# Narrow-head attention: scores made in rows for the maxima and again turned, from stacked high and low parts

## The chip, the cores and the metric

One core of a Trainium2 chip runs the whole network in one launch. The metric is device time in microseconds of one execution, the median of several. A profiled execution is one of them with the trace recorded.

## What is computed

x has 8 batches of 256 rows of 128 channels (2048 rows, 16 tiles of 128 rows, two tiles per batch); the context has 8 x 64 rows. Four layers follow each other, each an attention to the context and a feed-forward part. The change touches the attentions of layer 0 and layer 2, which have 16 narrow heads of 8 channels:

```python
q = split(layernorm(x) @ wq + bq)        # 16 heads of 8
k = split(ctx @ wk + bk); v = split(ctx @ wv + bv)
logits = einsum('bhqd,bhkd->bhqk', q, k) / sqrt(8) + mask * -1e9   # layer 2: no mask
out = einsum('bhqk,bhkd->bhqd', softmax(logits), v)
x = x + merge(out) @ wo + bo
```

Layer 0's mask is one 256 x 64 table for all batches and heads.

## The kernel before

The program is a row of stages (`nc.Block`). A block gives each engine (TensorE, VectorE, ScalarE, GpSimd, and SP, which issues DMAs) its own program, and ends with a barrier that all five pass together. Within a block engines meet by semaphores. Ahead of each narrow attention stand `normalise` (tag n) and, for layer 0 alone, a setup block (tag su) that turns the context and prepares masks. Then come two blocks.

`project_small` (tag p): TensorE makes K for all batches (`pk`, one 512-column product), V for all batches (`pv`) and Q in four groups of 512 rows (`pq`); ScalarE adds the biases and writes `kT_all` and `qT_all`, channels in partitions, and VectorE writes `v2_all`. SP has no program here.

`attend_small` (tag t) goes tile by tile, 16 tiles, in a loop of four with lags: step t makes scores of tile t, transposes those of t-1, multiplies those of t-2 with V, turns and projects the output of t-3, and adds it to x for t-4.

- GpSimd: once per batch the keys spread over 16 heads with zeros between (`kbd`, L352), per tile a copy of its q (`qs`, L357) and the output bias.
- TensorE: scores as two fp32 products of 512 columns (L374); eight transposes of 128x128 (L382) once the exponentials are there; the turn of the normalised output (L389); eight products with `vaug`, V with columns of ones for the denominators (L397); the output projection (L403). An fp32 product is two records in the trace.
- VectorE: in layer 0 scale and mask over 1024 scores per row (L467); maxima (L472); subtraction (L474); division by the denominators (L481, L483); addition to x (L460).
- ScalarE: exponentials (L435); copy of the transposed weights out of PSUM (L426); V placed in `vaug` (L421); the turned output (L431).

Ahead of the loop VectorE fills `vaug` (L443, L451), for which ScalarE waits, but not TensorE. During layer 0's attention SP loads the weights of the next parts (L2547).

Of the kernel before, what the change touches and what calls it, by code (L numbers as in the profile page):

```python
# [268 lines left out]
def project_small(nc, tag, w, zT, ctx2T, ident, qT_all, kT_all, v2_all):  # L269

    with ExitStack() as stack:
        m = Memory(nc, stack, tag)
        pq = [m.ps(f"pq{i}") for i in range(2)]
        pk = m.ps("pk")
        pv = m.ps("pv", 1024)
        q_done, q_out, k_done, v_done = m.sem("q_done"), m.sem("q_out"), m.sem("k_done"), m.sem("v_done")
        block = stack.enter_context(nc.Block())

        @block.tensor
        def _(pe):  # L280
            nc.tensor.matmul(pk[:, :].rearrange("p (b k) -> p b k", k=KEYS), w["wk"][:, :], ctx2T[:, :, 0, :],
                             start=True, stop=True).then_inc(k_done, 1)
            for b in range(B):
# [4 lines left out]
            for g in range(GROUPS):  # L288
                if g >= 2:
                    pe.wait_ge(q_out, g - 1)  # L290
                nc.tensor.matmul(pq[g % 2][:, :], w["wq"][:, :], zT[:, g * 512:(g + 1) * 512],
                                 start=True, stop=True).then_inc(q_done, 1)

        @block.scalar
        def _(act):
            act.wait_ge(k_done, 1)
            nc.scalar.activation(kT_all[:, :], pk[:, :], ACT.Identity, bias=w["bk"][:, 0:1])
            for g in range(GROUPS):
                act.wait_ge(q_done, g + 1)
                nc.scalar.activation(qT_all[:, g * 512:(g + 1) * 512], pq[g % 2][:, :], ACT.Identity,  # L300
                                     bias=w["bq"][:, 0:1]).then_inc(q_out, 1)

        @block.vector
        def _(dve):
            dve.wait_ge(v_done, 1)
# [4 lines left out]
def attend_small(nc, tag, x, w, qT_all, kT_all, v2_all, ident, headmask, scale, neg=None, loads=None):  # L310
# [2426 lines left out]
```

## Time and profile before

| | us |
|---|---|
| median of 3 executions | 1593.37 |
| lowest and highest | 1592.81, 1596.17 |
| the profiled execution | 1598.73 |
| its span in the trace | 1596.8 |
| layer 0: last K of the projection to last addition | 24.7 to 131.7 |
| layer 2: the same | 905.1 to 998.8 |

In the span TensorE is busy 1283.8 us (80%), its weight loads 1032.2, VectorE 1024.7 (64%), ScalarE 734.5 (46%), GpSimd 620.8 (39%). The share of an engine is an average over stages with different limits; the two stages in question are read from the timeline.

### The profile page before, as it was taken

How to read it: one execution, taken by the hardware profiler on the slowest of the kernel's cores; microseconds unless marked ns; L12 is line 12 of the kernel's file. 1: busy time of each engine (PE TensorE's matmuls, PEld its weight loads, DVE VectorE, ACT ScalarE, POOL GpSimd, SP SyncE). 2: the span in 40 equal slices, each digit the busy share in tenths (PEclk: the TensorE clock that was granted, in tenths of full speed). 3: DMA queues.
4: the chain of work that ended last, by engine and by line, in shares of the span. 5: the costliest groups of instructions: out<-in, count | busy, mean ns of one | idle time of the engine just before them, and what ended most of it. 6: DMA issues, size and time to landing. Idle time of an engine off the chain costs nothing. (4 is left out here: it accounts for less than half of the span.)

```text
span 1596.8 us, 24399 instructions
## 1 busy us (share of the span) xinstructions
PE 1283.8 (80%) x7148; PEld 1032.2 (65%) x7148; DVE 1024.7 (64%) x2047; ACT 734.5 (46%) x1260; POOL 620.8 (39%) x598
## 2 busy tenths in 40 slices
PE   4896669997997899721997499699946659999997
PEld 2673459987664599720886267588833438787875
DVE  3885678887324276660665466677768767667675
ACT  2443446665332554430654254455523325455553
POOL 1311634431000133245233131389844116676665
PEclk9996779999898899955999599699976669999998
DMA  3500011110000000131111100133202025343333
GB/s 89 143 0 1 0 41 36 39 39 5 1 0 0 20 1 0 60 112 55 35 48 32 44 1 0 45 97 97 95 19 103 1 60 125 109 130 115 126 115 104
DMA packets 69931, 85.64 MB, mean 54 GB/s; under 512 B 14282, under 2 KB 40269, under 8 KB 69850
## 3 DMA queue, kind: packets, MB, share of 16 engines
q1 hardware_dynamic: 67250, 79.94, 17.3%
q0 software_dynamic: 2272, 4.24, 0.8%
q10 hardware_dynamic: 336, 0.59, 0.2%
q8 instruction: 34, 0.56, 0.1%
q14 instruction: 39, 0.32, 0.1%
HBM read 69.98 MB, written 8.92 MB: 49 GB/s over the span
## 5 line engine op out<-in xcount | busy, mean ns | idle before, releaser
L2356 POOL TENSOR_TENSOR e_h<-e_h,e_gate 128x512 f32<-128x512 f32 x128 | 187.8, 1484 | 145.8 <-DVE e_h L2408 89.9
L2413 DVE TENSOR_TENSOR e_h_low<-e_h,e_h_high 128x512 fp32r<-128x512 f32 x132 | 117.8, 893 | 75.6 <-ACT e_h_high L2343 75.4
L2343 ACT ACTIVATE e_h_high<-e_h 128x512 fp32r<-128x512 f32 x132 | 83.5, 633 | 97.8 <-POOL e_h L2356 90.1
L228 PE MATMUL n_ps_t<-ident,n_zn 128*128 128x128 f32 x128 | 34.4, 433 | 90.5 <-DVE n_zn L167 82.7
L2408 DVE TENSOR_TENSOR e_h<-e_s,e_ps_b 128x512 f32<-128x512 f32 x132 | 89.4, 678 | 13.1 <-ACT e_s L2328 8.7
L1001 PE MATMUL u_ps_o<-u_vaug,u_pT 128*128 128x72 f32 x768 | 96.9, 269 | 0.0
L1001 PEld LDWEIGHTS u_ps_o<-u_vaug,u_pT 128*128 128x128 f32 x768 | 93.3, 192 | 0.0
L2328 ACT ACTIVATE e_s<-e_ps_a 128x512 f32<-128x512 f32 x132 | 77.7, 589 | 31.5 <-PE e_ps_a L1364 28.4
L228 PEld LDWEIGHTS n_ps_t<-ident,n_zn 128*128 128x128 f32 x128 | 23.9, 224 | 98.2 <-DVE n_zn L167 78.3
L932 POOL TENSOR_TENSOR u_kbd<-u_keys,groupmask 96x512 fp32r<-96x512 f32 x60 | 62.8, 1067 | 62.4 <-DMA u_keys<-s_k 37.2
L1028 ACT ACTIVATE u_sm<-u_sm 128x512 f32<-128x512 f32 x96 | 60.6, 631 | 54.5 <-DVE u_sm L1060 53.9
L1058 DVE TENSOR_REDUCE u_mx<-u_ps_s 128x2 f32<-128x512 f32 (+1 forms) x96 | 66.2, 690 | 20.0 <-PE u_ps_s L983 18.5
L1804 POOL DMA_INDIRECT sorted_y<-e_y,e_zb x39 | 37.8, 970 | 88.7 <-DVE e_y L2009 88.7
L1060 DVE TENSOR_TENSOR u_sm<-u_ps_s,u_mx 128x512 f32<-128x512 f32 x96 | 66.4, 692 | 7.1
L374 PE MATMUL t_ps_s<-t_kbd,t_qs 128*128 128x512 f32 x128 | 64.6, 632 | 6.5 <-POOL t_qs L357 6.5
L558 POOL MEMSET t_vbd<- 128x1024 f32 x1 | 1.0, 951 | 170.9 <-POOLq L495 170.9
L1580 ACT ACTIVATE e_s<-e_ps_a 128x512 f32<-128x512 f32 x64 | 38.3, 598 | 57.9 <-PE e_ps_a L1364 57.9
L397 PE MATMUL t_ps_o<-t_vaug,t_pT 128*128 128x72 f32 x512 | 64.2, 281 | 0.0
L397 PEld LDWEIGHTS t_ps_o<-t_vaug,t_pT 128*128 128x128 f32 x512 | 63.1, 201 | 0.0
L571 POOL TENSOR_TENSOR t_sm<-t_sm,t_den 128x1024 f32<-128x1024 f32 x16 | 30.4, 1901 | 82.3 <-DVE t_den L683 82.3
L1024 ACT ACTIVATE u_pT<-u_ps_t 128x512 f32<-128x512 f32 x96 | 57.0, 594 | 7.7 <-PE u_ps_t L989 6.0
L1362 PE MATMUL e_ps_y<-e_h_high,ed_low 128*128 128x512 f32 x132 | 52.9, 401 | 8.4 <-DVE e_y L2417 5.4
(439 smaller groups left out, 3901.3 us busy)
## 6 DMA issues: line engine op xcount, KB each, us to landing
e_gate<-gates_by_expert SPq DMA_DIRECT2D x256, 128.0 KB, 3.0
e_gate<-gates_by_expert SPq DMA_DIRECT2D x32, 256.0 KB, 3.4
w_raw<-in_L1w SPq DMA_DIRECT2D x24, 256.0 KB, 4.2
u_qs<-s_q SPq DMA_DIRECT2D x16, 192.0 KB, 2.6
u_keys<-s_k SPq DMA_DIRECT2D x8, 384.0 KB, 3.5
w_w<-in_L2w SPq DMA_DIRECT2D x24, 128.0 KB, 2.7
sorted<-blank SPq DMA_DIRECT2D x1, 2535.0 KB, 17.6
e_zb<-sorted SPq DMA_DIRECT2D x13, 195.0 KB, 2.5
```

What stands on the lines that cost most here:

```text
L374: last = nc.tensor.matmul(ps_s[p][:, h * 512:(h + 1) * 512], qs[p][:, :], kbd[r // 2][:, 8 * h:8 * h + 8, :].rearrange("p a b -> p (a b)") ...
L397: last = nc.tensor.matmul(ps_o[:, a * NA:(a + 1) * NA], pT[p][:, j, :], vaug[vb][:, a, pair * NA:(pair + 1) * NA], start=pair == 0, stop=p ...
L932: return eng.tensor_tensor(kbd[:, HG * g:HG * (g + 1), kb * P:(kb + 1) * P], keys[:, kb, g, :].unsqueeze(1).broadcast_to([ROWS, HG, P]), g ...
L1001: last = nc.tensor.matmul(ps_o[par][:, a * NA:(a + 1) * NA], pT[(r - 3) % 2][:, i, :], vaug[kb][:, a, own * NA:(own + 1) * NA], start=own ...
L1028: nc.scalar.activation(sm[r % 3][:, :], sm[r % 3][:, :], ACT.Exp, scale=scale).then_inc(p_ready, 1)
L1058: nc.vector.tensor_reduce(mx[r % 2][:, 0:heads], s3, X, ALU.max)
L1060: nc.vector.tensor_tensor(sm[r % 3][:, :].rearrange("p (h k) -> p h k", h=heads), s3, mx[r % 2][:, 0:heads].unsqueeze(2).broadcast_to([P, ...
L2328: nc.scalar.activation(s[c % 3][:, :], ps_a[c % 3][:, :], ACT.Silu).then_inc(s_ready, 1)
L2343: nc.scalar.activation(h_parts[k % 3][0][:, :], h[k % 3][:, :], ACT.Copy).then_inc(high_ready, 1)
L2356: nc.gpsimd.tensor_tensor(h[c % 3][:, :], h[c % 3][:, :], gate[pair % SLOTS][:, :], ALU.mult)\
L2408: nc.vector.tensor_tensor(h[c % 3][:, :], s[c % 3][:, :], ps_b[c % 3][:, :], ALU.mult)\
L2413: nc.vector.tensor_tensor(h_parts[k % 3][1][:, :], h[k % 3][:, :], h_parts[k % 3][0][:, :], ALU.subtract).then_inc(low_ready, 1)
```

## The change

**A stacked form of q and k** (new class `Stacked`). q and k are kept as a high part (fp32r) and a low part (what is left). In four subsets of four heads (32 channels), the stacked `q` holds in rows 0 to 95 high, high, low and the stacked `k` high, low, high, so that one fp32r product over 96 rows gives the score but for low times low. Rows 96 to 127 take the maxima of 16 heads, high and low part; the spread keys have -1 there at their own head (`takes`).

**project_small** computes the parts (ScalarE the high ones, VectorE the low ones), and SP copies them to their rows, 32 partitions at a time. Q is made ahead of V, in four PSUM banks.

**attend_small** goes by batches, eight and three rounds of lag, written out without a loop. Per batch: scores in rows (96 stacked rows) into two banks, maxima from there; the maxima split in two parts and turned by a product with the identity; ScalarE writes them in rows 96 to 127 of `st.q` for all four subsets; scores again, now with keys in the partitions and 256 queries in the columns, maxima included; the exponential goes from PSUM to `pT`, with no subtraction, no transposes and no copy. The mask of layer 0 is added by a product of its high and low parts with a stacked identity, ahead of each bank's scores. VectorE's preparation now also zeroes `mxs` and fills rows 96 to 127 of three `kbd` tiles, and TensorE waits for it.

```diff
+def project_small(nc, tag, w, zT, ctx2T, st, v2_all):
+        @block.sync
+            def restack(out, src, cols, row, there):
+                for s in range(SUBSETS):
+                    sp.dma_start(out[row:row + 32, s, cols].bitcast(F32), src[32 * s:32 * s + 32, cols].bitcast(F32))\
+                        .then_inc(there, 16)
+            every = slice(0, B * KEYS)
+            sp.wait_ge(k_high_ready, 1)
+            restack(st.k, st.k_high, every, 0, st.k_there)
+            restack(st.k, st.k_high, every, 64, st.k_there)
+            sp.wait_ge(k_low_ready, 1)
+            restack(st.k, st.k_low, every, 32, st.k_there)
+            for g in range(GROUPS):
+                cols = slice(g * 512, (g + 1) * 512)
+                sp.wait_ge(q_high_ready, g + 1)
+                restack(st.q, st.q_high, cols, 0, st.q_there[g])
+                restack(st.q, st.q_high, cols, 32, st.q_there[g])
+                sp.wait_ge(q_low_ready, g + 1)
+                restack(st.q, st.q_low, cols, 64, st.q_there[g])
...
+            def scores(b, t):
+                for h in range(2):
+                    wait(pe, mx_used, n - 1)
+                    if mask is not None:
+                        nc.tensor.matmul(ps_s[h][:, :], mask[0][:, t * P:(t + 1) * P], mask[1][:, :],
...
+                    for i in range(2):
+                        last = nc.tensor.matmul(ps_s[h][:, i * PAIR:(i + 1) * PAIR],
+                                                st.q[0:ROWS, s, b * PAIR + t * P:b * PAIR + (t + 1) * P],
+                                                kbd[b % 3][0:ROWS, s, :, :].rearrange("p h k -> p (h k)"),
...
+            def turned_scores(b, s):
+                if s == 0:
+                    pe.wait_ge(m_rows, b + 1)
+                wait(pe, p_ready, n - RING + 1)
...
+                for pair in range(2):
+                    last = nc.tensor.matmul(bank[:, pair * PAIR:(pair + 1) * PAIR],
+                                            kbd[b % 3][:, s, 2 * pair:2 * pair + 2, :].rearrange("p h k -> p (h k)"),
+                                            st.q[:, s, cols(b)], start=mask is None, stop=True, skip_group_check=True)
...
+            pe.wait_ge(zeroed, 1)
...
+            def exponentials(b, s):
+                act.wait_ge(st_done, n + 1)
+                nc.scalar.activation(pT[b % 2][:, 2 * s:2 * s + 2, :].rearrange("p a c -> p (a c)"), ps_t[n % RING][:, :],
+                                     ACT.Exp, scale=scale).then_inc(p_ready, 1)
...
+                if 0 <= b - 1 < B:
+                    place_values(b - 1)
+                    exponentials(b - 1, 0)
+                    exponentials(b - 1, 1)
+                    exponentials(b - 1, 2)
+                if 0 <= b - 2 < B:
+                    out_T(TPB * (b - 2))
+                if 0 <= b - 1 < B:
+                    exponentials(b - 1, 3)
...
+            for i in range(3):
+                last = nc.vector.tensor_copy(kbd[i][ROWS:P, :, :, :].rearrange("p s h k -> p (s h) k"),
+                                             takes[ROWS:P, :].unsqueeze(2).broadcast_to([P - ROWS, HEADS, KEYS]))
             last.then_inc(zeroed, 1)
```

SP's queue between the first loads and those of layer 0's attention. Before, the two batches of loads follow each other:

```order
L2547 DMA ctx_nat<-in_ctx 64x8x128
L98 UNCONDITIONAL_BRANCH
L341 UNCONDITIONAL_BRANCH [waits barrier_Pool_Activation_PE_DVE_SP_release]
L2547 DMA L0fwqkv<-in_L0fwqkv 128x384
L2547 DMA L0fwo<-in_L0fwo 128x128
```

Now the projection block stands between them, with these rows (the last four come four times, once per group of q):

```order
L98 UNCONDITIONAL_BRANCH
L304 UNCONDITIONAL_BRANCH [waits barrier_Pool_Activation_PE_DVE_SP_release]
L308 DMA a_k<-a_k_high 32x512 [waits p0_k_high_ready]
L308 DMA a_k<-a_k_high 32x512 x7
L308 DMA a_k<-a_k_low 32x512 [waits p0_k_low_ready]
L308 DMA a_k<-a_k_low 32x512 x3
L308 DMA a_q<-a_q_high 32x512 [waits p0_q_high_ready]
L308 DMA a_q<-a_q_high 32x512 x7
L308 DMA a_q<-a_q_low 32x512 [waits p0_q_low_ready]
L308 DMA a_q<-a_q_low 32x512 x3
```

Sixty DMAs were put ahead of the barrier into the attention, and the loads behind it.

TensorE in layer 0's attention, one tile in the steady part. Before:

```order
L374 MATMUL t_ps_s<-t_kbd,t_qs 128x512 [waits t0_s_used,t0_q_ready]
L374 MATMUL t_ps_s<-t_kbd,t_qs 128x512
L382 MATMUL t_ps_t<-ident,t_sm 128x128 [waits t0_pT_ready,t0_p_ready]
L382 MATMUL t_ps_t<-ident,t_sm 128x128 x7
L389 MATMUL t_ps_w<-ident,t_on 128x128 [waits t0_x_done,t0_on_ready]
L397 MATMUL t_ps_o<-t_vaug,t_pT 128x72 [waits t0_pT_ready]
L397 MATMUL t_ps_o<-t_vaug,t_pT 128x72 x7
L403 MATMUL t_ps_w<-L0wo,t_onT 128x128 [waits t0_onT_ready]
```

Now the second half of a round (one batch), from the second tile's scores in rows (L423 the mask, L427 the scores; L449 and L453 the same turned):

```order
L423 MATMUL t0_ps_s0<-wide_eye,hidesT 128x512 [waits t0_mx_used]
L427 MATMUL t0_ps_s0<-t0_kbd0,a0_q 128x256 x2
L423 MATMUL t0_ps_s1<-wide_eye,hidesT 128x512 [waits t0_mx_used]
L427 MATMUL t0_ps_s1<-t0_kbd0,a0_q 128x256 x2
L466 MATMUL t0_ps_o<-t0_vaug1,t0_pT1 128x72 [waits t0_p_ready,t0_on_ready]
L466 MATMUL t0_ps_o<-t0_vaug1,t0_pT1 128x72 [waits t0_p_ready] x7
L449 MATMUL t0_ps_t1<-hidesT,wide_eye 128x512 [waits t0_p_ready]
L453 MATMUL t0_ps_t1<-a0_q,t0_kbd2 128x256 x2
L474 MATMUL t0_ps_w<-ident,t0_on0 128x128 [waits t0_x_done,t0_on_ready]
L449 MATMUL t0_ps_t2<-hidesT,wide_eye 128x512 [waits t0_p_ready]
L453 MATMUL t0_ps_t2<-a0_q,t0_kbd2 128x256 x2
L478 MATMUL t0_ps_w<-L0wo,t0_onT0 128x128 [waits t0_onT_ready]
```

The transposes are gone, scores stand twice, and between the turn of the output (L474) and its projection (L478) stands one turned score.

VectorE at the head of layer 0's attention. Before two rows of memsets stand ahead of the first scores:

```order
L443 MEMSET t_vaug 128x704 x2
L451 MEMSET t_vaug 64x2 x16
L467 SCALAR_TENSOR_TENSOR t_sm<-t_ps_s,mask 128x1024 [waits t0_s_done]
L472 TENSOR_REDUCE t_mx<-t_sm 128x16
L474 TENSOR_TENSOR t_sm<-t_sm,t_mx 128x1024
```

Now:

```order
L561 MEMSET t0_zeros 128x256
L563 MEMSET t0_vaug0 128x704
L563 MEMSET t0_vaug1 128x704
L566 CAST t0_mxs0<-t0_zeros 128x256
L571 MEMSET t0_vaug0 64x2 x8
L566 CAST t0_mxs1<-t0_zeros 128x256
L571 MEMSET t0_vaug1 64x2 x8
L573 CAST t0_kbd0<-takes 32x1024
L573 CAST t0_kbd1<-takes 32x1024
L573 CAST t0_kbd2<-takes 32x1024
L580 TENSOR_REDUCE t0_mx0<-t0_ps_s0 128x8 [waits t0_nat_done]
```

Three key tiles, two tiles for the maxima and a tile of zeros were put ahead, and over the scores only the maxima are left.

## Rows read from the trace of the kernel before

**Rows 1.** Busy time by stretches: length, then PE, PEld, DVE, ACT, POOL, granted clock, DMA share, GB/s.

```profile
930.00:990.00 60.00, 59.59 (x398) 47.28 (x396) 41.87 (x65) 31.37 (x51) 17.03 (x27) 1.00 0.00 0
...
118.00:124.00 6.00, 5.26 (x27) 5.12 (x27) 0.64 (x3) 1.88 (x3) 0.00 (x0) 0.62 0.00 0
```

**Rows 2.** Timeline, layer 2's attention, TensorE: start, us, engine, line, op, names, count.

```profile
956.36 1.88 PE L374 MATMUL t_ps_s<-t_kbd,t_qs 128*128 128x512 f32 x4
...
958.08 1.04 PE L382 MATMUL t_ps_t<-ident,t_sm 128*128 128x128 f32 x8
...
959.07 1.90 PE L397 MATMUL t_ps_o<-t_vaug,t_pT 128*128 128x72 f32 x16
...
961.08 1.88 PE L374 MATMUL t_ps_s<-t_kbd,t_qs 128*128 128x512 f32 x4
```

**Rows 3.** Timeline, layer 0's attention, VectorE: the mask step of two tiles, eight apart.

```profile
68.87 1.23 DVE L467 SCALAR_TENSOR_TENSOR t_sm<-t_ps_s,mask 128x1024 f32<-128x1024 f32 x1 [0.75 <-PE t_ps_s L374]
...
109.04 1.23 DVE L467 SCALAR_TENSOR_TENSOR t_sm<-t_ps_s,mask 128x1024 f32<-128x1024 f32 x1 [0.74 <-PE t_ps_s L374]
```

**Rows 4.** Timeline, first scores and last addition of both attentions.

```profile
34.31 5.26 PE L374 MATMUL t_ps_s<-t_kbd,t_qs 128*128 128x512 f32 x8 [3.29 <-POOL t_qs L357]
...
131.43 0.29 DVE L460 TENSOR_TENSOR x<-x,t_ps_w 128x128 f32<-128x128 f32 x1 [1.79 <-PE t_ps_w L403]
...
914.75 5.37 PE L374 MATMUL t_ps_s<-t_kbd,t_qs 128*128 128x512 f32 x8 [3.21 <-POOL t_qs L357]
...
998.49 0.29 DVE L460 TENSOR_TENSOR x<-x,t_ps_w 128x128 f32<-128x128 f32 x1 [1.34 <-PE t_ps_w L403]
```

**Rows 5.** Timeline, ScalarE in both projection blocks: K, and the last Q.

```profile
24.04 0.69 ACT L297 ACTIVATE a_kT<-p_pk,L0bk 128x512 f32<-128x512 f32 x1 [2.38 <-PE p_pk L281]
...
31.06 0.69 ACT L300 ACTIVATE a_qT<-p_pq,L0bq 128x512 f32<-128x512 f32 x1 [0.17 <-PE p_pq L291]
...
904.44 0.69 ACT L297 ACTIVATE a_kT<-p_pk,L2bk 128x512 f32<-128x512 f32 x1 [2.38 <-PE p_pk L281]
...
911.58 0.69 ACT L300 ACTIVATE a_qT<-p_pq,L2bq 128x512 f32<-128x512 f32 x1 [0.17 <-PE p_pq L291]
```

**Rows 6.** Timeline, SP's queue: 1 row, 128 rows; then twice 96 rows of 4 bytes.

```profile
11.73 0.34 SPq L2547 DMA_DIRECT2D starts<-in_starts  x1
12.12 0.39 SPq L2547 DMA_DIRECT2D mask<-in_mask  x1
...
32.87 0.42 SPq L2547 DMA_DIRECT2D L0fqn<-in_L0fqn  x1
33.33 0.43 SPq L2547 DMA_DIRECT2D L0fkn<-in_L0fkn  x1
```

**Rows 7.** Timeline, fp32r products: 512 columns twice; then 256, 128, 256.

```profile
760.24 0.39 PE L1837 MATMUL e_ps_b<-w_high,e_z_low 128*128 x1
760.47 0.40 PE L1838 MATMUL e_ps_b<-w_low,e_z_high 128*128 x1
...
761.56 0.33 PE L1858 MATMUL e_ps_y<-w_down,e_h_high 128*128 x1
761.73 0.22 PE L1859 MATMUL e_ps_y<-w_down,e_h_low 128*128 x1
761.79 0.33 PE L1858 MATMUL e_ps_y<-w_down,e_h_high 128*128 x1
```

**Rows 8.** Timeline, VectorE: a 128x1024 step inside SBUF; the memsets of V.

```profile
19.30 0.69 DVE L2594 TENSOR_SCALAR neg<-mask 128x1024 bf16<-128x1024 uint8 x1
...
32.23 1.39 DVE L443 MEMSET t_vaug<- 128x704 f32 x2 [3.57 <-PEq L271]
```

**Rows 9.** Groups of instructions: line, names, shapes, count, busy, mean ns, idle before.

```profile
L932 POOL TENSOR_TENSOR u_kbd<-u_keys,groupmask 96x512 fp32r<-96x512 f32 x60 | 62.8, 1067 | 62.4 <-DMA u_keys<-s_k 37.2
...
L1028 ACT ACTIVATE u_sm<-u_sm 128x512 f32<-128x512 f32 x96 | 60.6, 631 | 54.5 <-DVE u_sm L1060 53.9
L1058 DVE TENSOR_REDUCE u_mx<-u_ps_s 128x2 f32<-128x512 f32 (+1 forms) x96 | 66.2, 690 | 20.0 <-PE u_ps_s L983 18.5
...
L431 ACT ACTIVATE t_onT<-t_ps_w 128x128 f32<-128x128 f32 x16 | 4.4, 272 | 8.7 <-PE t_ps_w L389 8.7
```

More of the change, by code:

```diff
@@ L282, in _ @@
                              start=True, stop=True).then_inc(k_done, 1)
+            for g in range(GROUPS):
+                nc.tensor.matmul(pq[g][:, :], w["wq"][:, :], zT[:, g * 512:(g + 1) * 512],
+                                 start=True, stop=True).then_inc(q_done, 1)
             for b in range(B):
@@ L287, in _ @@
             last.then_inc(v_done, 1)
[L288 to L292, printed above, removed]
         @block.scalar
@@ new lines, in values @@
+            def values(b, t):
+                n = TPB * b + t
+                if t == 0:
+                    pe.wait_ge(v_ready, b + 1)
+                wait(pe, on_ready, n)
+                for j in range(8):
+                    a, pair = j // 4, j % 4
+                    pe.wait_ge(p_ready, 4 * b + j // 2 + 1)
+                    last = nc.tensor.matmul(ps_o[:, a * NA:(a + 1) * NA],
+                                            pT[b % 2][:, j, t * P:(t + 1) * P], vaug[b % 2][:, a, pair * NA:(pair + 1) * NA],
+                                            start=pair == 0, stop=pair == 3)
+                last.then_inc(o_done, 1)
@@ new lines, in place_values @@
+            def place_values(b):
+                wait(act, o_done, TPB * (b - 1))
+                for half in range(2):
+                    rows = slice(64 * half, 64 * half + 64)
+                    out = vaug[b % 2][rows, :, :].rearrange("p a (j c) -> p (a j) c", c=NA + 2 * HD)
+                    src = v2_all[rows, b, :].rearrange("p (j e d) -> p j e d", e=2, d=HD)
+                    last = nc.scalar.activation(out[:, :, HD * half:HD * half + HD], src[:, :, half, :], ACT.Copy)
+                last.then_inc(v_ready, 1)
@@ new lines, in add @@
+            def add(n):
+                dve.wait_ge(w_done, n + 1)
+                dve.wait_ge(bias_added, n + 1)
+                nc.vector.tensor_tensor(x[:, n, :], x[:, n, :], ps_w[:, 0:P], ALU.add).then_inc(x_done, 1)
+            for b in range(B + 3):
+                if 0 <= b - 3 < B:
+                    add(TPB * (b - 3))
+                if b < B:
+                    maxima(b, 0)
+                if 0 <= b - 2 < B:
+                    divide(TPB * (b - 2))
+                if 0 <= b - 3 < B:
+                    add(TPB * (b - 3) + 1)
+                if b < B:
+                    maxima(b, 1)
+                    split_max(b)
+                if 0 <= b - 2 < B:
+                    divide(TPB * (b - 2) + 1)
@@ L2577, in _ @@
                 last.then_inc(turned, 1)
+                pe.wait_ge(hidden, 1)
+                for t in range(TPB):
+                    last = nc.tensor.transpose(ps_m[:, t * P:(t + 1) * P],
+                                               hides[:, t, :, :].rearrange("p a k -> p (a k)"), idn)
+                last.then_inc(hides_turned, 1)
             @block.scalar
@@ L2679, in lay_out @@
          "ident": np.eye(P, dtype=np.float32),
-         "headmask": np.repeat(np.eye(HEADS, dtype=np.float32), HD, axis=0),
+         "takes": np.concatenate([np.zeros((ROWS, HEADS), np.float32)] + 2 * [-np.eye(HEADS, dtype=np.float32)]),
+         "eye2": np.tile(np.eye(KEYS, dtype=np.float32), (2, 1)),
          "groupmask": np.tile(np.repeat(np.eye(HG, dtype=np.float32), HD, axis=0), (3, 1)),
```

331 lines of the change are left out of this document (184 added, 147 removed).

## The prediction

> **What bounds the kernel now.** I read first the busy time by stretches, then the timeline of the two attentions and of the small projections in front of them, then the groups of like instructions. The change touches two stages of a chain of stages separated by barriers, so what counts is the length of each stage, not the average over the kernel.
>
> In the L2 attention TensorE is the bound: in 930 to 990 us it is busy 59.59 of 60 us at the full clock, while VectorE has 41.87 and ScalarE 31.37 [rows 1]. The reader is to see one tile there: the scores start at 956.36, the eight transposes at 958.08, the eight products with V (16 records) with the output projection behind them at 959.07, the next scores at 961.08 [rows 2]. That is 1.72 for the scores, 0.99 for the transposes with the turn of the last output, 2.01 for values and projection: 4.72 us per tile, with nothing between. In the L0 attention the same TensorE work stands in a longer round: from the mask step of one tile at 68.87 to that eight tiles later at 109.04 is 40.17, 5.02 us per tile [rows 3]; the 0.3 more is TensorE waiting for VectorE, which there has a third pass of 1.22 us over the 1024 scores.
>
> From first score to last addition the L0 body runs 34.31 to 131.72, 97.4 us, and the L2 body 914.75 to 998.78, 84.0 us [rows 4]. Sixteen periods make 80.3 and 75.5; the rest, 17.1 and 8.5, is filling and draining. L0's rest is longer because its drain falls to the half clock (0.62 granted in 118 to 124 [rows 1]).
>
> The projection stage ahead is short: K is out of ScalarE at 24.73, the last Q at 31.75; in L2 905.13 and 912.27 [rows 5]. SP has nothing to do in it.
>
> **What is removed and added on TensorE.** Per tile the fp32 scores (1.72) and the transposes (0.88 of the 0.99) go; the values and the output stay. Per batch of two tiles come 16 fp32r matmuls of 256 columns (eight in rows for the maxima, eight turned), and two small turns of the maxima. The price of a 256-column fp32r matmul: 512 columns repeat after 0.23 (760.24 to 760.47), and a 256- and a 128-column one together after 0.23 (761.56 to 761.79) [rows 7]. 384 columns at 2.4 GHz are 0.16, so about 0.035 is added to each, and 256 columns cost 0.14; I take 0.15, with 0.13 and 0.17 as ends, since the stationary side changes at every one. A round (one batch) in L2 is then 16 x 0.15 = 2.40, turned maxima 0.22, values and projections 4.02, turns of the output 0.22: 6.86 us. L0 adds eight 512-column mask matmuls at 0.235, 1.88: 8.74 us.
>
> Waits inside the round. The even tile's projection stands behind its turn and one turned score, but on ScalarE the copy that it needs is queued behind the third exponential. That exponential starts 0.2 after turned score 2 ends and takes 0.63, the copy 0.27 [rows 9]: 1.13 with the handover. TensorE covers 0.11 + 0.30 of it (0.11 + 0.53 in L0): a wait of 0.72, 0.49 in L0. The odd tile's projection waits about 0.2 in L2. Rounds: 6.86 + 0.92 = 7.78 against 2 x 4.72 = 9.44 now, and 8.74 + 0.49 = 9.23 against 10.04. Nothing else ends later: VectorE has four maxima of 0.69, 0.65 for splitting them, 1.3 for dividing, 0.6 for adding, 5.3 per round; ScalarE four exponentials of 0.63, 1.05 for the maxima rows, 0.5 and 0.55, 4.6; GpSimd spreads one batch's keys in 2.1 (two of its 96x512 products [rows 9]) and adds two biases, about 3. The smaller of these figures are estimates from the same steps of today.
>
> Eight rounds are 62.2 and 73.8. Filling (scores, four maxima, split, turn, rows of maxima, first exponential) and draining add an estimated 6, the half clock of the first matmuls 1.8 (eight records took 5.26 where the full clock takes 3.4 [rows 4]), and in L0 2 more for a part of today's slow drain (0 to 9). Bodies: L2 70.0, so **14.0 less**; L0 83.6, so **13.8 less**.
>
> **What is added in front.** Before the first score TensorE now waits for VectorE's whole preparation: besides two memsets of V (1.39 together [rows 8]) and the ones (0.5), it fills zeros (0.3), two tiles from them (0.6) and three key tiles of 32x1024. The last have no row of their own; their ends are 0.69 (128x1024 to bf16 [rows 8]) and 1.22 (128x1024 out of PSUM [rows 3]), and I take 1.1 each, near the second, because the source is a broadcast. In sum 6.3 instead of 2.1: **+4.2 per attention**, ends 2.2 and 5.
>
> The page VectorE: DVE Perf Modes of the Trainium skill (the section on 2x mode with both ports) lets an fp32 copy inside SBUF run at twice the rate; by it the three would be 0.55 each and the sum 3.3 us less over both attentions. No row here has a copy of this shape.
>
> **The restack, the largest term.** SP now issues 60 DMAs of 32 rows in each projection block, 12 for the keys and 48 for the queries, and the block ends with a barrier that waits for SP as for every engine. What an issue costs is read off SP's queue: with 96 rows of 4 bytes the next follows after 0.46 (32.87 to 33.33), with a single row after 0.39 (11.73 to 12.12) [rows 6]; size hardly matters. For 32 rows I take 0.45, nearest the 96-row case, ends 0.38 and 0.47. SP starts when the keys' high part is out, 24.83, and stays the last engine: the last query part is computed by about 32, when SP has done sixteen. 60 x 0.45 = 27.0, so the block ends at 51.8 instead of 31.75: **+20.1**; in L2 at 932.2 instead of 912.27: **+20.0**. The GpSimd copies of q per tile that go were hidden. SP's weight loads for the next layer are now queued 20 us later (from 52, their last landing by about 87), well before 132, and hide.
>
> The page DMA: Bandwidth & Descriptors of the Trainium skill says, of the sequencer's dispatch, about 50 ns (Anatomy of one DMA), and that issuing is usually small relative to the DMA (Issuing engines are not separate DMA queues). By that, 60 issues would be 3 us and the block would hardly grow. The rows above say nine times as much, and I follow them; the rule is rival A.
>
> **Small things.** The setup block now has a second turn: mask transposed, copied by ScalarE behind its three copies (which end at 21.7), VectorE's low part behind that: **+1.0** (0.4 to 1.2). One more load in the first batch hides under the first normalisation.
>
> **The sum.** +20.1 + 20.0 + 8.4 + 1.0 - 13.8 - 14.0 = **+21.7 us**. The profiled execution took 1598.7 (span 1596.8); one like it would take 1620.4. Against the median of 1593.4 it is 1615.
>
> **Rivals.** *A, the issue is cheap.* If SP issued as fast as the parts are computed, each block would grow by about 1, and the sum is 2 + 8.4 + 1 - 27.8 = -16: **1577**. Against it stand all of SP's rows; the lowest is 0.39. The point from which it decides: the projection blocks may grow by 9.2 us each, that is 0.27 per issue. 10%.
>
> *B, the two cancel.* 0.38 per issue (-8.4) and no waits inside the rounds (-11): **1596**. It needs both, and the copy behind the third exponential stands in the order written. 8%.
>
> *C, the clock.* TensorE idles some 28 us before each attention and then 12% of each round; if it stayed at 1.2 GHz, its 6.86 and 8.74 would double, about +125: **1740**. For it: the drain in L0 fell to 0.62 at a busy share of about 0.87 [rows 1]. Against it: in L2 the same start after an idle stretch rose to the full clock within 3 us, and TensorE is now as dense as in L0. A fall in some rounds only gives tens of us. 4%.
>
> *D, the change does not do what it says* (the maxima and the mask go wrong in the split): it would alter values, not the order or sizes of instructions, and so no time. It has no share of its own.
>
> **How the numbers follow.** Forecast 1615 with 78%. Its own range: issue -8.4 to +2.4, preparation -4 to +2, fp32r matmuls -5 to +5, waits in the rounds -11 to +11, L0's drain -2 to +7. Not all at one end: 1598 to 1633. The chances left out are A, C and the tails of the forecast, about 2 in 10: 1597 to 1635. A measurement of this kernel tells about 0.2% (3.2 us) from no change. Slower: the forecast, C and half of B, 0.84. Same: half of B and the low tail, 0.06. Faster: A, 0.10.
>
> **What would show it.** SP's queue full from about 24.8 to 52 with 60 issues at 0.45, TensorE and VectorE idle at its end. The first score 6 us behind the barrier. A 256-column matmul repeating after 0.15. Rounds of 7.8 and 9.2 us, with the wait before the even tile's projection put down to ScalarE. I am wrong if issues of 32 rows take under 0.3, if rounds are over 9.4 in L2 (a new bound, or the clock), or if another engine ends the projection block.

## The result and the profile after

The changed kernel takes **1660.47 us** (median of 4 executions, 1655.23 to 1673.7) against 1594.25 of the kernel before on the same chip (4 executions, 1592.81 to 1596.17): a ratio of 1.0427, interval 1.0362 to 1.0493. It is slower by 66 us, where 21.7 were forecast, and lies outside the range of 1597 to 1635. The profiled execution has a span of 1662.1 us, 65.3 more than before, at a mean granted clock of 0.841 instead of 0.877. Of the variant e7 below, two of ten executions (1605.93 and 1606.93) were slow ones, more than 1.5% above its fastest; its median and ratio are those of the other eight, and its profile is of the first of the two.

First scores and last additions of both attentions, in the timeline of the changed kernel (start, us, engine, line, op, names); they answer to [rows 4]:

```profile
71.41 0.80 PE L423 MATMUL t_ps_s<-wide_eye,hidesT 128*128 128x512 f32 x1 [40.16 <-DVE t_kbd L573]
...
151.76 0.29 DVE L606 TENSOR_TENSOR x<-x,t_ps_w 128x128 f32<-128x128 f32 x1 [1.34 <-PE t_ps_w L478]
...
968.59 1.22 PE L427 MATMUL t_ps_s<-t_kbd,a_q 96*128 96x256 f32 x4 [39.82 <-DVE t_kbd L573]
...
1062.05 0.29 DVE L606 TENSOR_TENSOR x<-x,t_ps_w 128x128 f32<-128x128 f32 x1 [1.62 <-PE t_ps_w L478]
```

Layer 0's body, first score to last addition, is 80.6 us (97.4 before), and layer 2's is 93.7 (84.0 before). But the first scores come 37.1 us later in layer 0 and 53.8 later in layer 2. The 65.3 us divide by place: +20.3 to the end of layer 0's attention, -2.5 from there to the start of layer 2's K on ScalarE (922.27 against 904.44 [rows 5]), +36.0 from K to the first scores, +9.7 in layer 2's body, +1.7 behind it.

SP's queue in the projection block of layer 0, first and last copies and the first load of the next block; it answers to [rows 6], and the x8 and x4 are numbers of issues:

```profile
25.64 5.05 SPq L308 DMA_DIRECT2D a_k<-a_k_high  x8
30.74 2.49 SPq L308 DMA_DIRECT2D a_k<-a_k_low  x4
33.27 5.02 SPq L308 DMA_DIRECT2D a_q<-a_q_high  x8
...
61.47 2.49 SPq L308 DMA_DIRECT2D a_q<-a_q_low  x4
64.59 0.34 SPq L2685 DMA_DIRECT2D L0fwqkv<-in_L0fwqkv  x1
```

Eight issues, 30.74 - 25.64 = 5.10 us later the next: 0.64 each, where the loads that follow in the same queue go at 0.39 to 0.47. Behind the barrier comes VectorE's preparation, here its timeline with one product of GpSimd (POOL) that ran beside it:

```profile
64.73 0.27 DVE L561 MEMSET t_zeros<- 128x256 f32 x1 [32.22 <-PEq L294]
...
67.50 3.85 DVE L573 CAST t_kbd<-takes 32x1024 fp32r<-32x1024 f32 x3
67.60 2.34 POOL L407 TENSOR_TENSOR t_kbd<-a_k,groupmask 96x1024 fp32r<-96x1024 f32 x1
```

The three key tiles took 3.85 us, but one by one 0.69, 2.38 and 0.94 us: the first began ahead of GpSimd's product, the other two while GpSimd was at work.

The windows of both bodies (columns as in [rows 1]: length, then PE, PEld, DVE, ACT, POOL busy, granted clock, DMA share, GB/s):

```profile
80.00:90.00 10.00, 10.00 (x58) 9.20 (x57) 4.35 (x10) 5.00 (x9) 2.72 (x3) 0.75 1.19 252
90.00:100.00 10.00, 9.72 (x76) 9.06 (x76) 5.53 (x15) 4.14 (x9) 2.71 (x3) 1.00 0.40 61
...
1010.00:1020.00 10.00, 9.79 (x47) 9.49 (x45) 4.08 (x10) 3.47 (x6) 2.72 (x3) 0.50 0.00 1
1020.00:1030.00 10.00, 9.79 (x44) 9.26 (x44) 3.22 (x10) 3.23 (x8) 1.14 (x1) 0.50 0.00 0
1030.00:1040.00 10.00, 9.64 (x54) 9.20 (x52) 4.45 (x12) 3.66 (x9) 1.58 (x3) 0.63 0.01 2
1040.00:1050.00 10.00, 9.21 (x78) 8.80 (x78) 4.86 (x13) 5.75 (x12) 0.00 (x0) 1.00 0.00 1
```

In layer 0 the clock is back at its full level (1.00, 2.4 GHz) about 14 us after the first score. In layer 2, where it was full all through 930 to 990 before [rows 1], it is granted at 0.50 (1.2 GHz) for 69 us, although TensorE is busy 9.79 of 10 us in the steady part. A round there shows the price (additions of odd and even tiles, layer 2):

```profile
1010.32 0.29 DVE L606 TENSOR_TENSOR x<-x,t_ps_w 128x128 f32<-128x128 f32 x1 [0.75 <-PE t_ps_w L478]
1017.09 0.29 DVE L606 TENSOR_TENSOR x<-x,t_ps_w 128x128 f32<-128x128 f32 x1 [1.54 <-PE t_ps_w L478]
1023.06 0.29 DVE L606 TENSOR_TENSOR x<-x,t_ps_w 128x128 f32<-128x128 f32 x1 [0.75 <-PE t_ps_w L478]
1029.83 0.29 DVE L606 TENSOR_TENSOR x<-x,t_ps_w 128x128 f32<-128x128 f32 x1 [1.54 <-PE t_ps_w L478]
```

1017.09 to 1029.83 is 12.74 us per round, against 7.49 at the full clock (below, e10) and 8.87 in layer 0 (102.21 to 111.08). Once the clock is up, TensorE waits 0.51 us for ScalarE ahead of an even tile's projection:

```profile
1040.15 0.49 PE L478 MATMUL t_ps_w<-L2wo,t_onT 128*128 128x128 f32 x2 [0.51 <-ACT t_onT L541]
```

### The profile page after: what moved, and what is told of

It is laid out like the page before. It is cut to its first block and busy times, and to the rows that moved or that the text cites. A ratio compares the mean times of both kernels' runs of the same rounds, so it can differ in the third digit from the quotient of the medians.

```text
span 1662.1 us, 24143 instructions
## 1 busy us (share of the span) xinstructions
PE 1282.1 (77%) x7118; PEld 1055.1 (63%) x7118; DVE 995.0 (60%) x2089; ACT 722.9 (43%) x1277; POOL 614.7 (37%) x566
## 5 line engine op out<-in xcount | busy, mean ns | idle before, releaser
L2542 DVE TENSOR_TENSOR e_h_low<-e_h,e_h_high 128x512 fp32r<-128x512 f32 x132 | 117.7, 891 | 77.7 <-ACT e_h_high L2472 77.5
L407 POOL TENSOR_TENSOR t_kbd<-a_k,groupmask 96x1024 fp32r<-96x1024 f32 x16 | 31.2, 1950 | 213.5 <-PE t_ps_t L453 80.9
L2457 ACT ACTIVATE e_s<-e_ps_a 128x512 f32<-128x512 f32 x132 | 77.6, 588 | 25.4 <-PE e_ps_a L1493 22.8
L228 PEld LDWEIGHTS n_ps_t<-ident,n_zn 128*128 128x128 f32 x128 | 23.9, 224 | 97.6 <-DVE n_zn L167 77.5
L466 PE MATMUL t_ps_o<-t_vaug,t_pT 128*128 128x72 f32 x512 | 76.7, 315 | 0.0
L466 PEld LDWEIGHTS t_ps_o<-t_vaug,t_pT 128*128 128x128 f32 x512 | 75.1, 232 | 0.0
L517 ACT ACTIVATE a_q<-t_ps_m 32x1024 fp32r<-32x1024 f32 x16 | 16.3, 1017 | 110.7 <-PE t_ps_m L437 110.7
L1709 ACT ACTIVATE e_s<-e_ps_a 128x512 f32<-128x512 f32 x64 | 38.3, 599 | 58.2 <-PE e_ps_a L1493 58.2
L427 PE MATMUL t_ps_s<-t_kbd,a_q 96*128 96x256 f32 x128 | 32.3, 369 | 40.5 <-DVE t_kbd L573 39.8
```

Of the source, the lines that this page charges most:

```text
L228: last = nc.tensor.transpose(ps_t[g % 2][:, j * P:(j + 1) * P], normal(g * GROUP + j), ident)
L466: last = nc.tensor.matmul(ps_o[:, a * NA:(a + 1) * NA], pT[b % 2][:, j, t * P:(t + 1) * P], vaug[b % 2][:, a, pair * NA:(pair + 1) * NA], ...
L2457: nc.scalar.activation(s[c % 3][:, :], ps_a[c % 3][:, :], ACT.Silu).then_inc(s_ready, 1)
L2542: nc.vector.tensor_tensor(h_parts[k % 3][1][:, :], h[k % 3][:, :], h_parts[k % 3][0][:, :], ALU.subtract).then_inc(low_ready, 1)
```

## The experiments

Theory: the loss has two sources, the issue of 60 copies on one queue (some 31 us per block), and rounds that run at half clock in layer 2 (some 28 us). For the copies the rival is that they cost by bytes or landing. For the slow clock two causes were in question: the idle time in front, which was the theory when e2 was written, and the new rounds themselves, the theory from e5 on.

**e1, what an issue costs.** The kernel before, with a block at its very end that issues copies of several kinds, each series waited for.

```diff
+            for i in range(8):
+                sp.dma_start(zT[32 * (i % 4):32 * (i % 4) + 32, 512 * (i // 4):512 * (i // 4) + 512],
+                             a[32 * (i // 2 % 4):32 * (i // 2 % 4) + 32, 512 * (i % 4):512 * (i % 4) + 512])
+            ...
```

> The kernel before with a block behind its last stage in which SP issues series of copies, each series waited for before the next: inside SBUF 32 rows of 2 KB (8, partitions shifted as in the restack), 32 rows of 512 B (8), 32 rows of 8 KB (4), 128 rows of 2 KB (4), 64 rows of 2 KB (4), from DRAM 32 rows of 2 KB (8) and 128 rows of 2 KB (4), inside SBUF 16 rows of 2 KB (4); then ScalarE issues 8 of the first kind. In the changed kernel the restack's issues follow each other after 0.63 us, where the loads from DRAM of 1 to 128 rows follow after 0.39 to 0.47. Theory 'few rows' (32 rows cost more than 128): 0.63 for every series of 32 rows, DRAM too, 0.47 for 128 rows of either kind. Rival 'inside SBUF': 0.63 for all copies inside SBUF, 128 rows too, 0.47 for both series from DRAM. Rival 'size': the pitch grows with bytes, 32 rows of 512 B under 0.5, of 8 KB above 0.8.

SP's and then ScalarE's queue. In order: inside SBUF 32 rows of 2 KB, of 512 B, of 8 KB, 128 rows of 2 KB, 64 rows of 2 KB; from DRAM 32 rows and 128 rows of 2 KB; inside SBUF 16 rows of 2 KB; the first kind from ScalarE.

```profile
1588.20 5.62 SPq L2682 DMA_DIRECT2D zT<-z_high  x8
1595.42 4.94 SPq L2686 DMA_DIRECT2D zT<-z_high  x8
1601.54 3.31 SPq L2690 DMA_DIRECT2D zT<-z_high  x4
1608.42 2.47 SPq L2693 DMA_DIRECT2D zT<-z_high  x4
1612.82 2.41 SPq L2696 DMA_DIRECT2D zT<-z_high  x4
1617.01 3.60 SPq L2699 DMA_DIRECT2D zT<-in_x  x8
1622.21 1.77 SPq L2703 DMA_DIRECT2D zT<-in_x  x4
1628.14 2.45 SPq L2706 DMA_DIRECT2D zT<-z_high  x4
...
1632.39 5.08 ACTq L2713 DMA_DIRECT2D zT<-z_high  x8
```

Divided by their counts: inside SBUF 0.70, 0.62, 0.83, 0.62, 0.60 and 0.61 us, from ScalarE 0.64; from DRAM 0.45 and 0.44. So the theory named in the expectation, few rows, fell, and the rival "inside SBUF" held: what raises the price is the source, not the rows, and the bytes only at 8 KB per row (0.2 more). Why the first series took 0.70 and the same kind from ScalarE 0.64 stays open. The forecast's 0.45 was the right price for the wrong kind of transfer. The probe adds about 50 us by itself (1646.56 us in one execution), which says nothing more.

**e4, fewer issues, the same bytes.** All 2048 query columns in one copy per row block: 24 issues per attention instead of 60.

```diff
-            for g in range(GROUPS):
-                cols = slice(g * 512, (g + 1) * 512)
-                ...
+            cols = slice(0, TILES * P)
+            restack(st.q, st.q_high, cols, 0, st.q_there[0])
+            restack(st.q, st.q_high, cols, 32, st.q_there[0])
+            ...
```

> The changed kernel with each copy of q over all 2048 columns instead of four times 512: 24 issues per attention instead of 60, the same bytes. Theory (the price is per issue): each projection block ends 36 x 0.634 = 22.8 us earlier, but the last group of q must be computed first, which it is by the time the keys are issued: 1660 - 45 = 1615, less if the clock profits. Rival (the price is per byte or per descriptor): the issues of 8 KB per row take four times as long and nothing is gained.

Measured 1619.32 us (1618.4 to 1620.1), ratio 1.0144 [1.0123, 1.0165]. The first scores:

```profile
51.89 0.80 PE L422 MATMUL t_ps_s<-wide_eye,hidesT 128*128 128x512 f32 x1 [20.50 <-DVE t_kbd L572]
...
930.15 1.22 PE L426 MATMUL t_ps_s<-t_kbd,a_q 96*128 96x256 f32 x4 [21.20 <-DVE t_kbd L572]
```

Layer 0's come 19.5 us earlier than in the changed kernel with the same bytes moved. The number of issues is the larger part of what the block pays for. Bytes cost something too, which is why it is 19.5 and not 22.8: eight of the long copies, 8 KB per row, hold SP's queue for 7.36 us, 0.92 each:

```profile
33.23 7.36 SPq L308 DMA_DIRECT2D a_q<-a_q_high  x8
```

From K to the first scores layer 2 is 19.0 us shorter, and its body 5.4 shorter (88.4), because the half clock lasted 56 us instead of 69.

**e3, the same 60 issues beside the rounds.** They stand at the head of SP's program in the attend block, behind the barrier.

```diff
-        @block.sync
-        def _(sp):
-            ... (in project_small)
+        def restacks(sp):
+            ... (in attend_small, ahead of loads(sp))
+        block.sync(restacks)
```

> The changed kernel with the sixty restacking copies moved behind the barrier, to the head of SP's program in the attention block, ahead of the loads; GpSimd and TensorE wait for them by the semaphores that are there. Theory (the loss is in the barrier that waits for SP): the projection blocks end at about 33 us as before the change, and the first score waits only for the keys and the first group of queries, 24 issues at 0.63 and 2 us to land, 17 us after the block's start: the first score of layer 0 at about 50.5 instead of 71.4, of layer 2 21 us earlier too, the later groups arriving 7.6 us apart ahead of their use every 17 us. 1660 - 42 = 1618, and up to 25 less if the shorter idle stretch leaves the clock high. Rival (the copies are needed at once, so the stage moves with the data): the gain is under 15 us.

Measured 1618.22 us (1615.45 to 1623.62), ratio 1.014 [1.0108, 1.0172]. First scores at 49.41 and 936.48, waiting for the first query group's last copy and not for VectorE:

```profile
936.48 1.19 PE L424 MATMUL t_ps_s<-t_kbd,a_q 96*128 96x256 f32 x4 [18.18 <-DMA a_q<-a_q_low]
```

The later groups' copies, issued during the rounds, hold nothing up: layer 0's body is 79.9 us here. The front did what was expected, 21.6 us less in layer 0 and 21.1 in layer 2, counted from K to the first scores. That the whole, too, came out at the 1618 expected is partly luck: layer 2's body was 10.8 us shorter than in the changed kernel (half clock for 43 us instead of 69), and the self-attention behind layer 0 lost about as much (see e5).

**e2, no idle time in front.** Filler products keep TensorE busy while SP issues: 38 in each projection block and 7 ahead of the first scores.

```diff
+            for i in range(38):
+                nc.tensor.matmul(warm[:, :], w["wq"][:, :], zT[:, 0:512], start=True, stop=True)
```

> The changed kernel with TensorE kept busy where it waits: 38 products of 512 columns into a spare bank behind the projections (33 us at the full clock, SP still issues until then) and 7 ahead of the first scores. Nothing else changes. In the changed kernel's profile layer 2's attention ran at granted 0.50 for 65 us after an idle stretch, a round taking 12.7 us, where layer 0's rounds at 1.00 took 8.9. Theory clock (the idle stretch in front leaves the clock low, and that is the part of the loss in the body of layer 2): layer 2's body falls from 93.7 to 62 to 68 us and layer 0's from 80.6 to 74 to 78, the whole from 1660 to 1620 to 1632 us. Rival (the clock goes low because the rounds themselves are sparse): it falls again within the rounds and the whole gains under 10 us.

Measured 1652.49 us (1645.0 to 1661.03), ratio 1.037 [1.0334, 1.0406], 20 to 33 us above what was expected and within the rival's "under 10 us" of gain; the interval overlaps with that of the changed kernel. In layer 0 the clock stayed full (body 77.5 us). In layer 2 the fillers ended at 966.5 and the scores began at 967.24; the windows:

```profile
965.00:966.00 1.00, 1.00 (x4) 0.38 (x2) 1.00 (x2) 0.00 (x0) 1.00 (x2) 1.00 0.00 0
...
969.00:970.00 1.00, 0.63 (x4) 0.43 (x4) 1.00 (x3) 0.00 (x0) 0.76 (x2) 1.00 0.00 0
970.00:972.00 2.00, 1.65 (x6) 1.17 (x6) 1.83 (x5) 0.25 (x1) 0.00 (x0) 0.54 0.00 0
...
996.00:998.00 2.00, 2.00 (x14) 2.00 (x13) 1.41 (x3) 0.60 (x1) 0.00 (x0) 0.63 0.00 0
```

The clock fell just behind 970, in the first round, and came back only at 997. Layer 2's body was 77.2 us: 16.5 less than in the changed kernel, since 27 us at half clock are fewer than 69, but not the 62 to 68 expected. So idle time ahead is not what the slow rounds need, although less of them was slow without it: my theory of that moment, that the idle stretch costs the clock, fell, and the next runs were made for what is left.

**e8, the old rounds after the same idle time.** The kernel before, with 60 copies to a tile that nobody reads in each projection block; SP also waits there for the last to land.

```diff
+        @block.sync
+        def _(sp):
+            sp.wait_ge(k_out, 1)
+            for i in range(60):
+                ...
+                sp.dma_start(junk[32 * a:32 * a + 32, b * P:b * P + P], kT_all[32 * c:32 * c + 32, 0:P])
```

> The kernel before, both attentions old, with 60 copies of 32 rows (to a tile that nobody reads) issued by SyncE in each projection block, so that TensorE idles there as long as in the changed kernel. The idle alone: first scores 34 and 35 us later, 1663 us. Theory 1 (the new rounds' own stream keeps the clock low): the old rounds have full clock within about 10 us, the whole 1663 to 1668 us. Theory 2 (a long idle is followed by a long time at half clock whatever runs): layer 2's old rounds, which fill TensorE at full clock (10.00 of 10 us), stay at half clock for tens of us and take about twice 9.2 us: 1690 to 1700 us.

Measured 1665.65 us (1665.03, 1666.27), ratio 1.0438 [1.0411, 1.0464]: theory 1. Layer 2's first scores and windows:

```profile
980.52 5.93 PE L384 MATMUL t_ps_s<-t_kbd,t_qs 128*128 128x512 f32 x8 [35.78 <-POOL t_qs L367]
...
980.00:990.00 10.00, 7.92 (x19) 3.80 (x20) 5.22 (x20) 2.42 (x4) 6.65 (x11) 0.75 0.00 0
990.00:1000.00 10.00, 9.66 (x61) 7.12 (x60) 6.28 (x9) 6.23 (x11) 3.27 (x5) 1.00 0.01 2
```

After 35.8 us of idleness the old rounds have the full clock within 10 us, and the body (to the last addition at 1064.7) is 84.2 us, as before. In these rounds the idle time costs itself and nothing after it. The total fits in part by luck: the first scores came 32 us later in each attention instead of 34 and 35, layer 0's body was 4.6 us shorter, and the self-attention lost 6.6 (see e5).

**e6, layer 0's masking matmuls in layer 2.** The other side of the same question: the changed kernel, with a tile of zeros as a mask, in all eight rounds of layer 2.

```diff
+            attend_small(nc, "t2_", ..., mask=(nothing[:, :], ones_r[:, :]), masked=8)
```

> The changed kernel, with the masking matmuls that layer 0 has (one of 512 columns ahead of each bank's scores, here with zeros, which add nothing) put into layer 2 as well. Theory 1: what TensorE runs in the rounds decides when its clock comes back (layer 0 with these matmuls had it back 14 us after its first scores, layer 2 without them after 68): the half clock of layer 2 then ends within 10 to 20 us, rounds take 8.9 us as in layer 0, its body takes about 80 us instead of 93.7, and the whole 1645 to 1650 us. Theory 2: the place and what lay before it decide: the half clock lasts 60 us or more here too, rounds of about 15 us, body 105 to 115 us, the whole 1672 to 1682 us.

```profile
970.00:980.00 10.00, 2.47 (x7) 2.05 (x8) 7.54 (x26) 0.00 (x0) 9.48 (x9) 0.50 0.05 13
980.00:990.00 10.00, 8.75 (x40) 7.33 (x39) 5.41 (x12) 3.81 (x7) 0.85 (x2) 0.76 0.00 0
990.00:1000.00 10.00, 9.72 (x78) 9.16 (x76) 5.25 (x13) 4.88 (x9) 4.63 (x6) 1.00 0.01 2
```

Theory 1 again: with more work in every round the clock is back within the window 980 to 990, and layer 2's body is 78.9 us (977.5 to 1056.4), 15 shorter. The whole, 1657.05 us (1656.02, 1658.08), is above the 1645 to 1650 expected, because the profiled execution lost some 10 us between the two attentions (780.4 us from the last addition to K, 770.2 in the changed kernel; see e5).

**e5, only layer 0 changed.**

```diff
+            old_project_small(nc, "p2_", small2, zT, ctx2T, idn, qT_all, kT_all, v2_all)
+            old_attend_small(nc, "t2_", x, small2, qT_all, kT_all, v2_all, idn, headmask[:, :], HD ** -0.5)
```

> Only layer 0's attention is changed, layer 2's is the old one. If the two attentions are independent, as both theories have it for the front of the program, layer 0 keeps its +20.3 us of the changed kernel's span and layer 2 gives nothing: 1594.3 + 20 = about 1615 us. If something later than layer 0 (queues, clock) carries a part of the loss, it comes out away from that by more than 3 us.

Measured 1621.14 us (1616.22 to 1625.51), ratio 1.0149 [1.0114, 1.0184]: 6 above 1615, so the plain sum did not hold. In the profiled execution layer 0's attention ends 19.3 us later than before, and layer 2's old body takes its 84; but from layer 0's last addition to layer 2's K lie 780.1 us instead of 772.7. The loss is in the self-attention behind layer 0, which no edit touches. Its windows, some 94 to 104 us behind the end of layer 0's attention in each, in the kernel before and then in e6:

```profile
225.00:235.00 10.00, 10.00 (x87) 9.24 (x84) 8.65 (x14) 7.28 (x13) 6.11 (x6) 1.00 0.01 3
```

```profile
245.00:255.00 10.00, 10.00 (x46) 9.08 (x45) 4.46 (x7) 3.90 (x7) 3.06 (x4) 0.50 0.01 2
```

TensorE is full in both; once its clock is back, once it stays at 1.2 GHz for 20 us more. Six of the ten variants' profiles show the slow outcome here (e3, e5, e6, e7, e8, e10), and the kernel before, the changed kernel, e1, e2, e4 and e9 do not. As e8 has the old rounds in both attentions, the new rounds are not what it takes. The four executions of e5 fall in two pairs, 1616.22 and 1616.88, 1625.41 and 1625.51, and the profiled one is of the upper pair, so the same kernel may well go either way; only one of the four has a profile. What chooses stays open.

**e7, the front rebuilt.** Of the 60 copies 24 stay in the projection block, 14 from SP and 10 from ScalarE; 36 go beside the rounds; VectorE's preparation moves into the projection block.

```diff
+            act.wait_ge(k_low_ready, 1)
+            restack(act, st.k, st.k_low, every, 32, st.k_there)
...
+            restack(act, st.q, st.q_high, first, 32, st.q_there[0])
...
+            for g in range(1, GROUPS):   (head of SP's program in attend_small)
+                restack(sp, st.q, st.q_high, c, 0, st.q_there[g])
```

> The changed kernel with its front rebuilt: of the 60 copies only the keys' and the first query group's 24 stay in the projection block, 14 issued by SyncE and 10 by ScalarE; the other 36 go out at the head of SyncE's program beside the rounds; VectorE's preparation (zeros and key tiles) is done in the projection block while it waits for the queries. Theory of the issue price (0.63 us each, two queues at once): layer 0's first scores near 39 us instead of 71.4, layer 2's near 920 instead of 968.6; bodies 79.5 and 66 to 77 us by how long the half clock lasts; the last additions about 13 us (layer 0) and 16 to 27 us (both) ahead of the kernel before: 1567 to 1578 us. If the copies share one issuing path whichever engine issues them, the first scores come 5 us later in each and the whole is 1577 to 1588 us. If the landing of the later groups holds the rounds up, the rounds 2, 4 and 6 show waits for the query copies.

Measured 1589.68 us (8 executions, 1581.49 to 1603.17), ratio 0.9973 [0.9935, 1.0012], 12 to 23 us above what was expected. The front did what was expected: first scores at 36.69 and 910.16, before the 39 and 920. The two queues ran side by side, at 0.63 and 0.67 us per issue, and VectorE filled the three key tiles in 1.90 us instead of 3.85, with GpSimd idle:

```profile
25.04 5.03 SPq L295 DMA_DIRECT2D a_k<-a_k_high  x8
...
25.83 2.67 ACTq L295 DMA_DIRECT2D a_k<-a_k_low  x4
...
26.82 1.90 DVE L377 CAST a_kbd<-takes 32x1024 fp32r<-32x1024 f32 x3
```

Layer 0's attention ended 15.3 us ahead of the kernel before. In the profiled execution, one of the longest at 1605.93, the rest was lost to the clock: 70 us at half clock in layer 2 (body 95.1) and the slow outcome in the self-attention. The fastest execution, 1581.49, had a mean granted clock of 0.869 against its 0.851 and is near the forecast of 1578; how long layer 2 was slow in it no profile shows.

```profile
930.00:950.00 20.00, 19.57 (x89) 18.75 (x88) 7.12 (x19) 6.53 (x13) 5.43 (x6) 0.50 0.07 17
...
980.00:990.00 10.00, 9.36 (x77) 8.79 (x76) 6.17 (x18) 4.41 (x10) 0.00 (x0) 0.99 0.00 0
```

**e10 and e9, zero masks in the first three rounds of layer 2 only**, in the changed kernel (e10) and in the one with the rebuilt front (e9).

```diff
+                         mask=(nothing[:, :], ones_r[:, :]), masked=3)
...
+                mask = hide if b < masked else None
```

> The changed kernel with the zero masking matmuls in the first three rounds of layer 2 only. Theory 1: clock back about 14 us after the first scores, then rounds of 7.5 us: body 73 us instead of 93.7, the whole about 1640 us (1650 where the self-attention's half clock lasts longer). Theory 2: the half clock goes on past round 3 and the whole is 1655 us or more.

e10: 1646.85 us (1640.75 to 1652.24), ratio 1.0306 [1.0274, 1.0339], below the changed kernel's 1.0427 [1.0362, 1.0493] and between the two values expected; its profile has the slow outcome in the self-attention. The clock is full from the window 990 to 1000 on and stays so when the masks have stopped; body 71.8 us (978.4 to 1050.3). Rounds without masks at the full clock:

```profile
1013.91 0.29 DVE L617 TENSOR_TENSOR x<-x,t_ps_w 128x128 f32<-128x128 f32 x1 [1.00 <-PE t_ps_w L489]
1017.31 0.29 DVE L617 TENSOR_TENSOR x<-x,t_ps_w 128x128 f32<-128x128 f32 x1 [0.34 <-PE t_ps_w L489]
1021.40 0.29 DVE L617 TENSOR_TENSOR x<-x,t_ps_w 128x128 f32<-128x128 f32 x1 [1.00 <-PE t_ps_w L489]
```

> The kernel with the split front, with the zero masking matmuls in the first three rounds of layer 2 only. Theory 1 (the rounds' own stream keeps the half clock in layer 2, and these matmuls bring the full clock back): half clock in layer 2 ends within 20 us of the first scores at 910 instead of 65 us, the body takes 72 to 76 us instead of 95.1, the whole 1594.3 - 15 (layer 0) - 14 (layer 2) = about 1565 us, up to 1577 where the half clock of the self-attention behind layer 0 lasts the 20 us longer that it lasts in some executions; and the executions spread less than the 1581 to 1607 us without them. Theory 2 (all eight rounds need them): the clock stays at 0.50 once they stop, the whole about 1590 to 1600 us.

e9: **1579.84 us** (6 executions, 1575.46 to 1586.05), ratio 0.9903 [0.9876, 0.9929], 1% faster than the kernel before (1597.68 on this chip) and some 80 us faster than the changed one, which ran on another. Layer 0's attention ends at 118.9 (131.7 before) and layer 2's at 977.1 (998.8 before), its body 72.9 us:

```profile
910.00:920.00 10.00, 8.89 (x49) 8.04 (x49) 4.35 (x9) 5.33 (x10) 2.97 (x4) 0.69 0.38 93
920.00:930.00 10.00, 9.72 (x78) 9.12 (x76) 5.50 (x15) 5.23 (x11) 2.72 (x3) 1.00 0.30 74
...
976.79 0.29 DVE L629 TENSOR_TENSOR x<-x,t_ps_w 128x128 f32<-128x128 f32 x1 [1.34 <-PE t_ps_w L519]
```

The six executions spread over 11 us, the eight of e7 over 22. It missed the expected 1565 by 15. The main parts are 3.4 because the kernel before was that much slower on this chip than the 1594.3 counted from, 2.2 because layer 0's part came to -12.8 instead of -15 with first scores at 38.05, and 5 because layer 2's, from K to the last addition, came to -9.0 instead of -14. The median lies 3 us above the profiled execution (1576.71, span 1574.9), and what the median one lost no profile shows.

## Why the prediction was wrong, point by point

- **The direction was right, the size was a third.** Slower by 66 us, not by 21.7.
- **The issue price, the largest term, was mis-sized.** The step "For 32 rows I take 0.45, nearest the 96-row case" failed. The copies cost 0.64 each (61.47 + 2.49 less 25.64, over 60), outside its ends of 0.38 and 0.47. From K to the first scores layer 2 grew by 36.0 us instead of 24.2: 31.4 for the restack, 4.6 for VectorE. The rows used were loads from DRAM; e1 shows that the source decides. The mechanism (60 issues in series, SP the last engine at the barrier, first scores behind it) held, as e3 and e4 show: 11.4 us too few in each block, 23 in all. The sentence of the Trainium skill's page DMA: Bandwidth & Descriptors on dispatch (Anatomy of one DMA, about 50 ns) was further off still, as the forecast had said, and rival A with it: 60 issues would be 3 us by it, an estimate, and they held the queue for 38.3. That section is on transfers which GpSimd issues, and so was no price for SP's queue.
- **The clock, rival C, came true in part.** The sentence that failed is "Against it: in L2 the same start after an idle stretch rose to the full clock within 3 us, and TensorE is now as dense as in L0". The first half is true of the old rounds, and e8 shows a rise within 10 us even after 36 us of idleness; it said nothing of the new ones. The second half was no ground either: layer 2's new rounds, which lack the mask matmuls of layer 0, kept TensorE busy 9.79 of 10 us and stayed at half clock. Layer 2's body was 93.7 us instead of 70.0, +23.7; at 12.74 us per round instead of 7.49, 69 us at half clock cost 69 x (1 - 7.49/12.74) = 28 us, an estimate. The forecast's own sign, rounds of layer 2 over 9.4 us by a new bound or the clock, had come. "A fall in some rounds only gives tens of us" named the size, but it got no part of the range: the two together, 23 + 24, less the 3 by which layer 0's body was the shorter, are the 43.6 us by which the span missed the sum.
- **The rounds were right.** 8.87 us in layer 0 (9.23 forecast) and 7.49 in layer 2 at the full clock (7.78), both with the wait for ScalarE before the even tile's projection: 0.27 us in L0 and 0.51 in L2 (its row at 1040.15), where 0.49 and 0.72 were forecast. Layer 0's body was 80.6 (83.6 forecast). Layer 2's without what the half clock cost, 93.7 - 28 = some 66, would have been 4 below the forecast.
- **VectorE's preparation came out right by luck, the setup was right.** 64.73 to 71.35 is 6.6 us (6.3), the key tiles 3.85 in all (3.3). But a tile was priced at 1.1, and one by one they took 0.69, 2.38 and 0.94: too high a price and the loss beside GpSimd, which the forecast did not have, nearly cancel. In e3, where GpSimd is idle at that time, all three took 1.90 and the preparation 4.7 us. In L0 the projection's first product comes 0.9 us later (1.0).
- **The 2x rule is closer than the price taken.** The Trainium skill, VectorE: DVE Perf Modes (Mode 2×_2P), has an fp32 copy inside SBUF at twice the rate; the 0.55 per tile that the forecast worked out by it, an estimate, is nearer to the 0.68 of e3, e7 and e9 than the 1.1 taken.
- **A rest of -0.8 us** is the sum of the stretches between and behind the two attentions (-2.5 and +1.7).

## What to carry to other kernels

Price an issue by a row with the same source and destination: here a copy inside SBUF of up to 2 KB per row held its queue 0.60 to 0.70 us whatever its rows, a load from DRAM 0.45, so copies go in as few issues as their order allows, over two queues, and beside the rounds, not ahead of a barrier. When rounds are rewritten, ask how long the new ones may run at the lower clock, since neither an idle stretch ahead nor TensorE's busy share was a measure of it here, and give a rise that comes late its own share of the range. A few products added only where the clock is low can pay for themselves: with them layer 2's body was 22 us shorter, their own time included (e10 against the changed kernel, e9 against e7).

## What the runs showed of the hardware

- Copies inside SBUF cost their queue 0.60 to 0.70 us up to 2 KB per row and 0.83 (e1) to 0.95 (e4) at 8 KB, from DRAM 0.44 and 0.45 (e1); ScalarE's queue issues at nearly SP's rate and at the same time (0.67 and 0.63, e7).
- A stream that keeps TensorE busy 9.79 of 10 us ran at 1.2 GHz for 69, 70, 56 and 43 us (changed kernel, e7, e4, e3; idle in front 39.8, 5.1, 21.2 and 18.2 us) and for 27 after a fall in its first round (e2), and then rose without any change in it. With one more 512-column product per bank in the first rounds it was back for good within 6 to 14 us each time (e6, e9, e10, and layer 0 of every variant that has the new rounds, but for e2, where it never fell). Whether the kind of these products, their length or the small gaps that they fill brings the clock back was not separated.
- The clock stays up afterwards at busy shares of 9.2 and 8.6 of 10 us (changed kernel, 1040 to 1060), lower than those at which it had stayed down.
- In the self-attention behind layer 0 a TensorE without a gap (10.00 of 10) is granted the full clock in some profiled executions and half of it, for 20 us more, in others.
- The same 32x1024 copy on VectorE took 0.68 to 0.69 us with GpSimd idle (e3, e7, e9), and up to 2.38 beside GpSimd's product of 96x1024, which took 2.34 instead of 1.88 itself (changed kernel). No run was made for this pair alone.
